# Weight addresses on TensorE in pairs and ahead of the wait, in the wide stages of a four-layer megakernel

## The reference, cut to what matters

```python
x = x + conv(_ln_c(x))
t = _to_tokens(x)                       # 16 images of 24 x 24: 9216 tokens of 64 channels
logits = _ln_t(t) @ router_w.T          # 8 experts
topk_probs, topk_idx = jax.lax.top_k(jax.nn.softmax(logits), 2)
gates = topk_probs / (topk_probs.sum(-1, keepdims=True) + 1e-09), placed by expert
h1 = jnp.einsum('nc,ehc->neh', flat, w1)
h3 = jnp.einsum('nc,ehc->neh', flat, w3)
h = silu(h1) * h3
y = jnp.einsum('neh,ech->nec', h, w2)
t = t + jnp.einsum('ne,nec->nc', gates, y)
```

## Time and profile before

| | |
|---|---|
| median of three runs | 2027.19 us (2026.78 to 2030.93) |
| profiled execution, its own time | 2032.62 us |
| its span, first to last instruction | 2030.8 us |
| granted TensorE clock, mean over the span | 0.826 |
| busy share of the span: TensorE, VectorE, ScalarE, GpSimd | 72%, 83%, 63%, 46% |
| chain of waits by engine: TensorE, VectorE, ScalarE | 37%, 17%, 2% |
| first up product to last tile reduction, layer 2 | 1054.2 to 1398.8 us |
| first up product to last tile reduction, layer 3 | 1658.9 to 2005.1 us |

### The profile page before, as it was taken

The page is one execution under the profiler, slowest core; times in us unless marked ns, Lnnn a source line. Parts: engine busy times, 40 slices in busy tenths (PEclk is TensorE's granted clock), DMA queues, the critical chain, the costliest instruction groups (busy, mean ns, idle before and its releaser), DMA issues.

```text
span 2030.8 us, 47407 instructions
## 1 busy us (share of the span) xinstructions
PE 1452.7 (72%) x16020; PEld 1087.5 (54%) x16020; DVE 1687.7 (83%) x2922; ACT 1281.8 (63%) x2367; POOL 938.8 (46%) x899
## 2 busy tenths in 40 slices
PE   3648899526777776688349999995331449999994
PEld 2545444515333343344248888884221248888884
DVE  5676888697778858888669999999868769999998
ACT  1026899212999967499228888886320138888883
POOL 1003778100233311167027777656216757777653
PEclk9756999575999967699559999997655669999997
DMA  8000000000000100000001111210300011111212
GB/s 324 1 0 29 2 29 2 0 0 0 29 29 29 57 1 1 1 22 27 8 15 42 42 41 42 81 32 8 130 0 18 22 32 43 42 41 41 79 33 99
DMA packets 49470, 74.98 MB, mean 37 GB/s; under 512 B 13636, under 2 KB 34235, under 8 KB 46590
## 3 DMA queue, kind: packets, MB, share of 16 engines
q1 hardware_dynamic: 28354, 42.26, 6.5%
q0 software_dynamic: 20896, 29.73, 4.3%
HBM read 39.88 MB, written 33.08 MB: 36 GB/s over the span
## 4 chain that ended last, share of the span: by engine, by line
PE 37%; DVE 17%; issue 4%; ACT 2%; DMA 0%; POOLq 0%; POOL 0%; DVEq 0%; SPq 0%; ACTq 0%
PE bank L1843 13%; PE bank L1844 11%; PE bank L1860 5%; PE bank L1862 3%; DVE tmp L1181 2%; DVE x L1483 2%; PE bank L1715 1%; PE bank L1564 1%; PE bank L1814 1%; DVE xn L1003 1%; DVE st L1001 1%; DVE tmp L1154 1%; ACT hl L868 1%; DVE xn L1022 1%; DVE st L1002 1%
## 5 line engine op out<-in xcount | busy, mean ns | idle before, releaser
L689 POOL TENSOR_TENSOR x<-x,ysb 128x256 f32<-128x256 f32 x248 | 232.8, 939 | 620.9 <-DVE ysb L1489 603.6
L636 POOL DMA_INDIRECT rows<-rowsb,pos x288 | 306.7, 1065 | 205.7 <-DVE pos L1310 119.2
L868 ACT ACTIVATE hb<-bank,bias_sb 128x512 f32<-128x512 f32 x432 | 315.2, 730 | 85.0 <-issue 42.0
L675 POOL DMA_INDIRECT y<-w,ids x256 | 283.8, 1109 | 136.2 <-DVE w L1381 71.5
L1843 PE MATMUL bank<-xT,uA_ 128*114 128x256 f16 x960 | 258.0, 285 | 5.3
L1843 PE MATMUL bank<-xT,gA_ 128*114 128x256 f16 x960 | 251.2, 286 | 5.9 <-issue 3.6
L1844 PE MATMUL bank<-xT,uB_ 128*114 128x256 f16 x960 | 253.3, 278 | 0.0
L1391 DVE TENSOR_TENSOR act<-bank,act 114x512 f32<-114x512 f32 x320 | 219.8, 687 | 36.0 <-PE bank L1844 16.6
L885 ACT ACTIVATE act<-bank 114x512 f32<-114x512 f32 x320 | 191.2, 597 | 81.6 <-PE bank L1844 67.2
L1844 PE MATMUL bank<-xT,gB_ 128*114 128x256 f16 x960 | 242.3, 275 | 0.0
L1860 PE MATMUL bank<-dW_,hl 114*128 x1920 | 229.1, 220 | 3.1 <-DVE hl L1395 3.1
(11 more groups left out here) (389 smaller groups left out, 3461.8 us busy)
## 6 DMA issues: line engine op xcount, KB each, us to landing
stage<-up SPq DMA_DIRECT2D x8, 1368.0 KB, 7.1
xs<-rows SPq DMA_DIRECT2D x160, 65.0 KB
rows<-land POOLq DMA_DIRECT2D x8, 1137.5 KB, 16.7
rows<-rowsb,pos POOLq DMA_INDIRECT x288
y<-w,ids POOLq DMA_INDIRECT x256, 2.3
stage<-down SPq DMA_DIRECT2D x2, 1368.0 KB
rowsb<-y SPq DMA_DIRECT2D x4, 640.0 KB, 6.2
x<-tokens SPq DMA_DIRECT2D x2, 1152.0 KB, 7.1
```

The source lines that it names most:

```text
L636: pool.indirect_dma_start(rows_d[l - SPARSE], bass.IndirectOffsetOnAxis(pos[h][:, k, j:j + 1], 0), words(h)[:, j * RW // 2:(j + 1) * RW // ...
L675: pool.indirect_dma_start(y_d, bass.IndirectOffsetOnAxis(ids[:, t * SUB + u:t * SUB + u + 1], 0), ysb[r][:, u * C:(u + 1) * C], None, boun ...
L689: pool.tensor_tensor(xv, xv, tg[u % 2], ALU.add).then_inc(s["added"], 1)
L868: ins = a.activation(dst[:, 0:SPAN * P], PB[w % 3][:, :], ACT.Gelu, scale=1.0 / WSCALE, bias=b1T[l][:, at:at + 1])
```

## The change

For a chunk's product pair (high and low weight of the same half), a new function asks for both addresses before either product is written, and ahead of the wait. Since the two register additions then stand next to each other, they merge into one fused instruction. The waits on s_ready and prod_ready, asked for behind it, land on the first product; for down products both halves' addresses come ahead of the wait on hp_ready.

```diff
+                def addresses(*parts):
+
+                    for part in parts:
+                        pe.lower_ap(part, for_matmul_weights=part.shape[1] == CH)
+
                 def up23(i, k, g, ahead):
...
-                        wait_from(pe, s[freed], i * (UNROLL * g_) + (gb + q - 1))
                         for c in range(2):
                             o = slice(c * ROWS, (c + 1) * ROWS)
-                            pe.matmul(PB[bank][0:CH, o], w[0][2 * g + c][:, at], xT[k][:, :], start=True, stop=False)
-                            ins = pe.matmul(PB[bank][0:CH, o], w[1][2 * g + c][:, at], xT[k][:, :], start=False, stop=True)
+                            high, low = w[0][2 * g + c][:, at], w[1][2 * g + c][:, at]
+                            addresses(high, low)
+                            if c == 0:
+                                wait_from(pe, s[freed], i * (UNROLL * g_) + (gb + q - 1))
+                            pe.matmul(PB[bank][0:CH, o], high, xT[k][:, :], start=True, stop=False)
+                            ins = pe.matmul(PB[bank][0:CH, o], low, xT[k][:, :], start=False, stop=True)
...
                 def down23(i, k, g):
 
-
+                    at = ds(bases[i * UNROLL + k, 1], 2 * C)
+                    down = [dW[2 * g + c][:, at] for c in range(2)]
+                    addresses(*down)
                     pe.wait_ge(s["hp_ready"], i * (UNROLL * SPLIT) + (split_base(l) + k * SPLIT + g + 1))
                     y = PB[4 + k % 2]
-                    at = ds(bases[i * UNROLL + k, 1], 2 * C)
                     for c in range(2):
-                        w = dW[2 * g + c][:, at]
+                        w = down[c]
```

## The result

The changed kernel takes **1975.68 us** (median of four runs, 1974.10 to 1978.38) against 2026.99 us of the kernel before on the same chip: a ratio of 0.9734 (95% interval 0.9713 to 0.9756), 51.3 us less.

The account below looks back on a forecast made before the run. TensorE was taken to pace the wide stages, with VectorE next at 3.945 us a tile. Terms 3.0 + 5.75 + 33.9 - 2 - 2 = 38.65 us, off 2027.19, gave 1988.5 us, range 1981 to 2010.

Parts of the forecast that it names:

- 33.9 - 2: Tiles 27 to 79 of both wide stages: 33.9 us gained at 0.32 a tile, 2 given back to other VectorE work.
- The asides of layer 3: Three pieces of other work between VectorE's products in layer 3, now counting in full: 2 us back, 0 to 3.6.
- The settling and the load of the expert word: TensorE's sequencer working out the next tile's expert and loading expert numbers: 0.27 us lost a tile.
- the place of the waits: Waits moved from address instruction to product on TensorE: worth nothing today, since TensorE waits for none of the three.
- the lead does not build: Rival: addressed products cost TensorE's sequencer nearly the array's time, so the 0.27 us stays; about 2004 us, chance 0.17.
- the pair costs more: Rival: a fused address instruction takes 90 ns and the sequencer binds, 62 us slower: 2089 us, chance 0.04.
- a lead that is lost where the work is long: Register work on TensorE's sequencer is free when it is ahead of the array, and otherwise costs its whole length.
- the stop at tile 29: TensorE stops some 5.6 us (layer 2) and 2.9 us (layer 3) at tile 29's transposes, until its rows are loaded.
- GpSimd's scatter follows its own queue, which the change does not speed up: Step: the scatter that tile 29's load waits for ends no earlier, cutting the 8.6 us gain of tiles 0 to 26.
- 3.0 + 5.75 us: Gain kept up to tile 29's transposes: 3.0 us in layer 2 (1.6 to 3.5), 5.75 in layer 3 (4.35 to 6.25).
- 2 off for the clock: TensorE's clock granted at 0.50 after each stop at tile 29: 1 us lost for each, 0 to 2.
- The 2.2 us that the prediction took for the landing: Assumed time from issuing tile 29's 65 KB row load to its landing, in both wide stages: 2.2 us.

Follow-up runs that it names:

- e5: Kernel before with the address pair in the down products alone, waits unmoved: 1986.58 us, ratio 0.9800.
- e10: Kernel before with the address pairs in the up products alone, waits unmoved: 1978.62 us, ratio 0.9729.
- e4: Kernel before with all tiles of a stage on the first tile's expert: 1979.65 us, ratio 0.9755.
- e6: Changed kernel with six more register instructions in every chunk, for down products with addresses of their own: 2090.27 us, ratio 1.0311.
- e7: Changed kernel with 6 in place of 10 scatter rows between two outputs on GpSimd's queue, so a later scatter: 2005.08 us, ratio 0.9888.
- e13: Kernel before with VectorE's subtraction on half of its columns behind the first four tiles of a stage: 2029.12 us, ratio 0.9992.
- e14: Kernel before with VectorE's product on half of its columns: 2030.13 us, ratio 0.9986.
- e9: Changed kernel with VectorE's product on half of its columns: 1963.15 us, ratio 0.9653.
- e1: Kernel before, unchanged, profiled a second time: 2029.62 us, ratio 0.9989.
- e12: Changed kernel, unchanged, run and profiled once more: 1979.53 us, ratio 0.9734.

## Why the prediction was right and where it was wrong

**Right: what paced the stage, and what paces it now.** TensorE's sequencer was the bound through its register instructions (e5, e10 and, with none left, e4); with fewer of them VectorE is, at 3.93 us a tile against the 3.945 that the prediction took from the tail of layer 3. From the reduction of tile 27 to that of tile 79 the two stages lost 217.71 - 200.84 = 16.9 and 219.38 - 204.79 = 14.6 us, 31.5 together; the prediction's terms there were 33.9 - 2 = 31.9. The asides of layer 3 give back 2.3 us (the stages' difference in that stretch went from 1.7 to 3.95), for which it took 2.

**Right in sign, wrong in size, without effect.** The settling and the load of the expert word come to an estimated 0.31 + 0.09 = 0.40 us a tile, not 0.27; a register instruction takes the sequencer 0.1 us or more, not the 32 to 42 ns of its record; and the place of the waits, priced at nothing, is worth 0.09 us a tile on its own, since one semaphore instruction a tile goes with it. None of it reached the sum, since VectorE stops the gain long before. For the same reason the rivals "the lead does not build" and "the pair costs more" could not win: a pair's record is 37 ns, and a pair replaces two instructions of 0.1 us. But the prediction's picture, a lead that is lost where the work is long, was too kind to the single additions: e6 shows that 35 instructions bind the whole tile.

**Wrong: the stop at tile 29.** The step that failed is "GpSimd's scatter follows its own queue, which the change does not speed up". It kept 3.0 + 5.75 us of the first 27 tiles and took 2 off for the clock. Measured at the transposes of tile 29: 115.80 - 106.07 = 9.73 and 115.73 - 105.93 = 9.80 us, and no fall of the clock. That is 6.73 + 4.05 + 2 = 12.8 us more; 38.65 + 12.8 = 51.4, and 51.3 were measured. Of the 12.8 us, this step is 2 x 8.64 - 8.75 + 2 = 10.5: without the stop the prediction's own 0.32 us a tile would have kept 8.64 in each layer. The other 2.3 lie in the gain of a tile: these first 27 gained 0.36 us each in place of 0.32. The mechanism of the stop is real (e7: 11.2 us of stop, clock 0.50, and 12.6 to 12.9 us a stage), and it was in the right place. It did not come because VectorE's subtraction holds GpSimd's transfers less often in the changed kernel, so that the load was issued 6.6 and 4.1 us earlier behind the first up product. That the subtraction holds them is shown (e13, e14); why it does so less often at the new pace is argued. The prediction named "if GpSimd's scatter ends at another time" as a sign of being wrong, but no term of its sum and none of its chances had a scatter that moves; even its best end, 44.8 us, keeps the stop.

That the earlier end just sufficed is luck. The room at tile 29 was no more than 0.10 and 0.15 us; the second profile of the changed kernel stops for 0.8, since its load took 3.22 us to land, and e9, faster by 0.12 us a tile, stops for 2.0 and 1.7. The 2.2 us that the prediction took for the landing was no part of the error: over the profiles the last part lands 1.7 to 3.2 us behind the issue. Nor is the issue itself fixed: in layer 3 of the kernel before it came 107.78 us behind the first up product in one profile and 111.19 in the other (e1), so that the 5.75 us kept there rest on one execution.

## What to carry to other kernels

Where an engine is busy without waiting for anyone and still slower than its work, count the instructions on its sequencer, register and semaphore instructions alike, and price them by the spacing of what they stand between, not by their records; merging neighbours is then worth a whole instruction each, up to the pace of the next engine, read where that engine was once late. When a change makes one engine steadier, look also at the queues that share something with it: here transfers on GpSimd got shorter because fewer of them began in a VectorE instruction with two SBUF inputs. And a wait that a faster kernel ought to run into is worth an experiment that forces it: it shows the price, and how near it is. Last, count in the trace what an edit took away: e4 was to remove one kind of register instruction and removed them all.

## What the runs showed of the hardware that was not expected

- A register instruction of 32 to 42 ns by its record costs TensorE's sequencer 0.1 us or more: at least 0.30 us for three (e5), and starts never less than 0.112 us apart from one address to the next.
- A GpSimd indirect transfer takes 0.96 us, or until 0.83 us behind the end of a VectorE subtraction with both inputs in SBUF in which it began (725 of the 741 that began with over 0.135 us to go, over the sixteen profiles; the other 16 began less than 0.04 us behind the subtraction's start), up to 1.45 us in the kernel before; a VectorE product with one input in PSUM does not hold it.
- VectorE's records can grow while its pace stays: L1391 has 0.68 us in the earlier trace rows, 0.72 at 1102 us of the changed kernel and 762 ns in the mean of its group on the page of the changed kernel, all with the next instruction 0.60 us later. The second profile of the same kernel (e12) has 677 ns at the same pace, so it is not the lack of a gap that makes them grow; what does is open. Where an engine has no gap, its pace is to be read from starts.

```profile
L1391 DVE TENSOR_TENSOR act<-bank,act 114x512 f32<-114x512 f32 x320 | 243.8, 762 | 12.4 <-PE bank L1852 12.4
...
L1391 DVE TENSOR_TENSOR act<-bank,act 114x512 f32<-114x512 f32 x320 | 216.8, 677 | 12.8 <-PE bank L1852 11.7
```
